# A half tile of keys whose rounded part and rest share one product, with the odd last key added by VectorE

## The chip, the cores and the metric

The kernel runs on one core of a Trainium2 chip. Its time is device time in microseconds (us), the median of several executions. Lower is better.

## What is computed

A gated block: cross-attention of 4 x 256 tokens over 1601 context rows of 256 features, then a feed-forward part in fp8 (e4m3).

```python
scores = einsum('bsd,bmd->bsm', layernorm(x), ctx) / sqrt(256)      # b=4, s=256, m=1601, d=256
scores = where(mask, scores, -1e30)
x = x + tanh(g_xattn) * (softmax(scores) @ ctx)                     # zero where no key is allowed
gate, up = e4m3(layernorm(x)) @ e4m3(w_gating[0]), ... @ e4m3(w_gating[1])   # 256 -> 1024
x = x + tanh(g_ffn) * (e4m3(gelu(gate) * up) @ e4m3(w_linear))      # 1024 -> 256
```

## The kernel before

Each batch element `b` has two tiles of 128 queries, so there are eight query tiles `j` (0 to 7, `b = j // 2`). The 1601 keys are 12 full tiles of 128 and a tail of 65, padded to 66. Four full tiles make a group `g` (0, 1, 2); the tail is group 3. To keep float32 accuracy at the speed of the rounded type fp32r, each operand is split in a rounded part (hi) and a rest (lo), and each product is made of three: hi x hi, hi x lo and lo x hi.

Each engine runs a list of steps written out by hand, one string per engine, `PE_ORDER` and its like (lines 56 to 100). `SP_ORDER` is the order of the loads on SyncE's DMA queue, and `BANK_ORDER` gives each transposing step one of three PSUM banks (`ring`) in turn. The steps are:

- `C b:i` turns the context of batch `b` (keys on partitions) into `cT` (features on partitions): TensorE transposes into a ring bank (line 773), ScalarE writes the rounded part (line 512), VectorE the rest (line 645). `C b:6` is the tail: two transposes of a 66 x 128 block. Some `C` steps of batches 2 and 3 are turned by VectorE instead (steps `D`, line 639). `X` does the same for the normalised queries.
- `A` and `S` are the score products (lines 787 to 808), `M` on VectorE adds the mask and takes the maximum (line 660), `E` on ScalarE is the exponential over all 1601 keys with its sum (line 527).
- `P j:g` transposes the weights of softmax, group by group (line 773), and splits them into `pT_hi` and `pT_lo`. `P j:3` is the tail: one transpose of a 128 x 65 block.
- `R` (ScalarE, line 519) and `Z` (GpSimd, line 461) split the context itself into hi and lo (`chl`).
- `V j:g` (`weigh`, lines 815 to 835) accumulates weights times context in PSUM (`pv`): per key tile one product of each kind, lines 824, 828 and 832. `V j:3` is the tail: three products with 65 rows of contraction.
- `A j` on VectorE (`add_attention`, lines 665 to 679) scales `pv` and adds it to `x` (line 678). `V j+1:0` waits for it (`pv_used`), since there is one `pv`.
- `B 0:g` spreads the first batch's mask over the partitions: a product with one row of contraction (line 744).
- `U`, `Q`, `L`, `N` are the second layernorm: VectorE, GpSimd (lines 451 to 454), ScalarE (line 560) and TensorE with ScalarE (lines 771 and 567). `H` are the 16 products of the first feed-forward layer (line 853) with gelu (line 575) and the multiplication (line 692), `Y` the eight of the second (line 869), each followed by line 697 and a store.
- `W` and `I` round the weights of the feed-forward part (VectorE, GpSimd).

The built program marks each product with the part of TensorE's array that it uses. Those of line 744, with one row, carry 32 x 128; all others, those with 65 and 66 rows and the transposes of 65 columns too, carry 128 x 128.

Of the kernel before, what the change touches and what calls it, by code (L numbers as in the profile page):

```python
# [5 lines left out]
def gated_cross_attention_ffn(  # L6
# [25 lines left out]
    TAIL = K - NF * P  # L32
    TPAD = TAIL + TAIL % 2
    KPAD = NF * P + TPAD
    GT = 4
# [21 lines left out]
        X0:0 W2 C0:0 W2 X0:1 C0:1 W2 A0:0 A1:0 C0:2 C0:3 A1:1 C0:4 A0:1 C0:5 B0:1 S0:1 C0:6 B0:2 B0:0 S1:1  # L57
        B0:3 C1:0 C1:1 S0:2 S0:3 X1 C1:3 S1:2 S1:3 C1:2 C1:4 C1:5 S2:0 S3:0 P0:1 P0:2 P0:0 S2:1 P1:1 P1:0
        C1:6 V0:0 S3:1 V0:1 P0:3 P1:3 V0:2 S2:2 X2 V0:3 P1:2 S2:3 V1:0 V1:1 S3:2 S3:3 S4:0 P2:1 V1:2 P2:2
        S5:0 V1:3 P2:0 C2:6 S4:1 S5:1 P3:0 P3:3 P3:1 V2:0 V2:1 P2:3 S4:2 X3 V2:2 V2:3 P3:2 S4:3 S5:2 S5:3  # L60
        V3:0 V3:1 P4:0 V3:2 V3:3 P4:2 C3:6 S6:0 P4:1 V4:0 S6:1 V4:1 P4:3 V4:2 P5:3 S6:2 S6:3 P5:1 P5:0 V4:3
        S7:0 S7:1 P5:2 S7:2 S7:3 P6:3 N0 V5:0 V5:1 N1 P6:1 P6:0 V5:2 V5:3 P6:2 P7:0 V6:0 P7:1 H0 V6:1 V6:2
        V6:3 H1 P7:2 P7:3 V7:0 V7:1 V7:2 V7:3 H2 N2 H3 H4 H5 H6 N3 H7 H8 H9 H10 H11 Y0 H12 Y1 H13 H14 H15 Y2
# [23 lines left out]
        F0 B0 Z0:0 Z0:3 F1 Z0:2 Z0:1 F3 Z1:3 Z1:1 F2 I0 Z1:2 I1 Z1:0 I2 Z2:1 Z2:3 Z2:0 Z2:2 Z3:2 Q1 Z3:3 Q0  # L87
        Z3:1 Z3:0 I3 I4 Q2 Q3 I5"""
# [828 lines left out]
```

## Time and profile before

| | us |
|---|---|
| median of 3 executions | 126.16 |
| lowest and highest | 125.7, 126.9 |
| the profiled execution | 126.15 |
| its span, first to last instruction | 124.4 |
| TensorE busy in it | 120.5 (97%) |
| VectorE busy | 97.1 (78%) |
| ScalarE busy | 87.7 (71%) |
| GpSimd busy | 82.5 (66%) |

The granted TensorE clock was 1.000 over the whole span. PE is TensorE's multiplying, PEld its loading of stationary operands, which normally runs beside the product in front. DVE is VectorE, ACT ScalarE, POOL GpSimd, SP SyncE. The record of one product is longer than the pace at which products follow each other, since they are pipelined; so durations of TensorE are read here as distances, from the chain of work, and not as mean lengths of records.

### The profile page before, as it was taken

The numbers are of one execution on the slowest core, as the hardware profiler recorded it, in microseconds if no ns is written. First come the engines' busy times: TensorE is split into PE (matmuls) and PEld (weight loads), VectorE is DVE, ScalarE is ACT, GpSimd is POOL, SyncE is SP. The second block draws the span as 40 slices with busy tenths as digits, with TensorE's granted clock in tenths as the row PEclk, the third lists the DMA queues.
The fourth block names the chain that finished last, engine by engine and source line by source line (L and its number), as shares of the span: only waits on it lengthen the run. The fifth ranks groups of instructions, "written<-read, shape, count | busy, mean of one in ns | idle before, by whom it ended". The sixth has DMA issues, their size and how long they took to land.

```text
span 124.4 us, 2562 instructions
## 1 busy us (share of the span) xinstructions
PE 120.5 (97%) x860; PEld 104.3 (84%) x860; DVE 97.1 (78%) x210; ACT 87.7 (71%) x155; POOL 82.5 (66%) x143
## 2 busy tenths in 40 slices
PE   6999999999999999999999999999999999999991
PEld 4798689887999998899999999899988984355780
DVE  3656699899999999997997796792778967666661
ACT  4288999996959969959867987969572339872400
POOL 3399399692995999199995984969519817920000
DMA  3959798679959999689717100000140000001133
GB/s 97 319 201 329 286 313 263 110 131 373 196 81 234 119 362 165 94 123 330 234 31 122 21 0 0 3 5 0 12 156 0 5 0 0 3 0 47 42 127 127
DMA packets 34439, 15.73 MB, mean 127 GB/s; under 512 B 26229, under 2 KB 33018, under 8 KB 34426
## 3 DMA queue, kind: packets, MB, share of 16 engines
q1 hardware_dynamic: 34424, 15.57, 49.5%
q8 instruction: 7, 0.11, 0.4%
q14 instruction: 6, 0.05, 0.2%
q10 hardware_dynamic: 2, 0.00, 0.0%
HBM read 14.52 MB, written 1.05 MB: 125 GB/s over the span
## 4 chain that ended last, share of the span: by engine, by line
PE 93%; ACT 3%; DVE 1%; issue 1%; ACTq 0%
PE ring L773 16%; PE pv L824 10%; PE pv L832 10%; PE pv L828 10%; PE scores L787 9%; PE scores L791 9%; PE scores L790 9%; PE scores L853 6%; PE ring L869 6%; PE pv L813 3%; ACT gate L575 2%; ACT x2T L567 1%; PE ring L744 1%; PE scores L808 1%; PE scores L804 1%; PE scores L807 1%
## 5 line engine op out<-in xcount | busy, mean ns | idle before, releaser
L461 POOL TENSOR_TENSOR chl<-cn,chl 128x256 fp32r<-128x256 f32 (+1 forms) x52 | 37.5, 754 | 5.0 <-ACT chl L519 5.0
L645 DVE TENSOR_TENSOR pT_lo<-ring,pT_hi 128x512 fp32r<-128x512 f32 (+1 forms) x32 | 18.0, 579 | 4.6 <-ACT pT_hi L512 4.4
L512 ACT ACTIVATE pT_hi<-ring 128x512 fp32r<-128x512 f32 (+1 forms) x32 | 15.5, 511 | 8.0 <-PE ring L773 8.0
L645 DVE TENSOR_TENSOR cT_lo<-ring,cT_hi 128x512 fp32r<-128x512 f32 (+1 forms) x28 | 17.0, 629 | 4.9 <-ACT cT_hi L512 4.6
L469 POOL TENSOR_TENSOR ws<-ws,wc 128x256 f32<-128x256 f32 x24 | 15.4, 678 | 7.9 <-DVE wc L687 7.9
L791 PE MATMUL scores<-cT_hi,xT_lo 128*128 128x512 f32 (+2 forms) x60 | 20.1, 342 | 0.0
L790 PE MATMUL scores<-cT_lo,xT_hi 128*128 128x512 f32 (+2 forms) x60 | 20.0, 342 | 0.0
L824 PE MATMUL pv<-chl,pT_hi 128*128 128x256 f32 (+1 forms) x104 | 18.9, 294 | 0.0
L832 PE MATMUL pv<-chl,pT_lo 128*128 128x256 f32 (+1 forms) x104 | 17.5, 281 | 0.0
L828 PE MATMUL pv<-chl,pT_hi 128*128 128x256 f32 (+1 forms) x104 | 17.4, 280 | 0.0
L787 PE MATMUL scores<-cT_hi,xT_hi 128*128 128x512 f32 (+2 forms) x60 | 16.9, 363 | 0.0
L512 ACT ACTIVATE cT_hi<-ring 128x512 fp32r<-128x512 f32 (+1 forms) x28 | 14.7, 548 | 2.9 <-PE ring L773 1.9
L472 POOL TENSOR_TENSOR wq<-ws,wc 128x256 bf16<-128x256 f32 x24 | 15.4, 672 | 0.5
L773 PE MATMUL ring<-ident,sp 128*128 128x128 f32 (+1 forms) x104 | 15.2, 273 | 0.0
L824 PEld LDWEIGHTS pv<-chl,pT_hi 128*128 128x128 f32 (+1 forms) x104 | 14.7, 189 | 0.4
L828 PEld LDWEIGHTS pv<-chl,pT_hi 128*128 128x128 f32 (+1 forms) x104 | 14.6, 189 | 0.0
L832 PEld LDWEIGHTS pv<-chl,pT_lo 128*128 128x128 f32 (+1 forms) x104 | 14.5, 188 | 0.0
L519 ACT ACTIVATE chl<-cn 128x1024 fp32r<-128x1024 f32 (+1 forms) x16 | 13.9, 892 | 0.7 <-PE pv L832 0.7
L527 ACT ACTIVATE sp<-sp,nb,sr 128x1601 f32<-128x1601 f32 x8 | 13.8, 1729 | 0.3
L773 PEld LDWEIGHTS ring<-ident,sp 128*128 128x128 f32 (+1 forms) x104 | 12.1, 140 | 1.4 <-DVE pT_lo L645 0.5
L791 PEld LDWEIGHTS scores<-cT_hi,xT_lo 128*128 128x128 f32 x60 | 11.3, 188 | 1.3
L790 PEld LDWEIGHTS scores<-cT_lo,xT_hi 128*128 128x128 f32 x60 | 11.3, 188 | 1.2
(85 smaller groups left out, 210.4 us busy)
## 6 DMA issues: line engine op xcount, KB each, us to landing
cn<-in_ctx_dram SPq DMA_DIRECT2D x11, 512.0 KB, 6.2
ws<-in_L_ffn_w_gating_dram SPq DMA_DIRECT2D x4, 512.0 KB, 4.4
raw<-in_ctx_dram SPq DMA_DIRECT2D x24, 64.0 KB, 3.0
act<-in_ctx_dram SPq DMA_DIRECT2D x24, 64.0 KB, 3.7
ws<-in_L_ffn_w_linear_dram SPq DMA_DIRECT2D x2, 512.0 KB, 4.1
out_dram<-xs SPq DMA_DIRECT2D x8, 128.0 KB, 1.7
mrow<-in_mask_BxS_bk_dram SPq DMA_DIRECT2D x3, 200.1 KB, 5.6
cn<-in_ctx_dram SPq DMA_DIRECT2D x2, 256.0 KB, 3.3
```

What stands on the lines that cost most here:

```text
L461: last = nc.gpsimd.tensor_tensor(chl[b % 2][0:parts, t, D:2 * D], cn[b % 2][0:parts, t, :], chl[b % 2][0:parts, t, 0:D].bitcast(f32), ALU. ...
L469: last = nc.gpsimd.tensor_tensor(ws[:, i % 2, c], ws[:, i % 2, c], wc[:, c], ALU.add)
L472: last = nc.gpsimd.tensor_tensor(wq[:, i, c], ws[:, i % 2, c], wc[:, c], ALU.subtract)
L512: nc.scalar.activation(dst, bank_view(f, size), ACT.Copy).then_inc(hi_ready, 1)
L645: nc.vector.tensor_tensor(dst, bank_view(f, size), hi.bitcast(f32), ALU.subtract).then_inc(lo_ready, 1)
L773: last = nc.tensor.transpose(dst, src, ident[0:parts, 0:parts])
L787: nc.tensor.matmul(dst, xT_hi[:, j % (2 * QT), k, :], cT_hi[:, k, cols], start=(k == 0), stop=False)
L790: nc.tensor.matmul(dst, xT_hi[:, j % (2 * QT), k, :], cT_lo[:, k, cols], start=False, stop=False)
L791: last = nc.tensor.matmul(dst, xT_lo[:, j % (2 * QT), k, :], cT_hi[:, k, cols], start=False, stop=(k == KD - 1))
L824: nc.tensor.matmul(pv[:, 0:D], hi[0:parts, t, :], chl[b % 2][0:parts, t, 0:D], start=(t == 0), stop=False)
L828: nc.tensor.matmul(pv[:, 0:D], hi[0:parts, t, :], chl[b % 2][0:parts, t, D:2 * D], start=False, stop=False)
L832: last = nc.tensor.matmul(pv[:, 0:D], lo[0:parts, t, :], chl[b % 2][0:parts, t, 0:D], start=False, stop=(t == NT - 1))
```

## The change

The tail's 65 keys are taken as 64 and 1.

- **The 64 keys.** `P j:3` transposes 128 x 64. The rounded weights go to partitions 0 to 63 of one block and the rest to partitions 64 to 127 of the same block. `R` rounds 128 partitions of the tail, and the load brings the 64 context rows twice, to partitions 0 to 63 and 64 to 127. `V j:3` is now two products: one with 64 rows of contraction (hi x lo), one with 128 rows, in which the hi and lo weights stand under each other against the doubled rounded context.
- **The odd key.** Its context row lies on all partitions in `crow` (steps `O` on SyncE's queue, and a first small load on ScalarE's). After each exponential ScalarE copies the odd key's weight to `podd`. `A j` gets a VectorE instruction in front of its last one, which adds `podd` times `crow` to `pv`.
- **The scores** still want `cT` of 66 columns: `C b:6` is now four transposes, two of 64 rows and two of 2 rows (odd key and a copy), in the order 64, 2, 64, 2.
- Two memsets of VectorE go. Some small tensors share memory with others.
- All orders are redrawn. The steps are the same but for the new `O0` to `O3` on SyncE's queue. The four `B0` steps now stand in four places of TensorE's order; before, two of them were neighbours.

```diff
     PE_ORDER = """
-        X0:0 W2 C0:0 W2 X0:1 C0:1 W2 A0:0 A1:0 C0:2 C0:3 A1:1 C0:4 A0:1 C0:5 B0:1 S0:1 C0:6 B0:2 B0:0 S1:1
-        B0:3 C1:0 C1:1 S0:2 S0:3 X1 C1:3 S1:2 S1:3 C1:2 C1:4 C1:5 S2:0 S3:0 P0:1 P0:2 P0:0 S2:1 P1:1 P1:0
...
+        X0:0 W2 C0:0 C0:1 W2 X0:1 W2 A0:0 A1:0 C0:3 C0:2 A1:1 B0:1 A0:1 B0:0 C0:5 C0:6 S0:1 C0:4 B0:2 S1:1
+        X1 C1:2 S0:2 B0:3 S0:3 C1:3 C1:1 C1:0 S1:2 S1:3 C1:5 C1:4 S2:0 S2:1 P0:0 P0:1 P1:1 S3:0 V0:0 C1:6
+        P0:3 P1:0 S3:1 P0:2 S2:2 S2:3 V0:1 P1:2 S3:2 V0:2 V0:3 S3:3 X2 P2:0 V1:0 P1:3 V1:1 P2:3 S4:0 V1:2
+        V1:3 P2:2 S5:0 S4:1 S5:1 C2:6 P2:1 P3:0 P3:1 V2:0 P3:2 S4:2 X3 S4:3 V2:1 V2:2 V2:3 S5:2 P3:3 S5:3
+        V3:0 V3:1 V3:2 P4:0 V3:3 S6:0 P4:1 S6:1 P4:2 V4:0 P4:3 V4:1 C3:6 V4:2 V4:3 P5:1 S6:2 S6:3 P5:3 P5:2
...
     SP_ORDER = """
-        X1 C1:0 C1:3 C1:1 C1:2 C2:3 X2 W0 M1 C2:0 T2:0 W1 C2:2 C2:1 T2:1 C3:1 C3:3 T2:2 C3:2 W2 M2 T3:0 T3:1
-        W3 C3:0 M3 W4 T3:2 W5"""
+        X1 W0 C1:3 C1:1 O1 C1:0 C1:2 M1 X2 C2:0 T2:0 C2:3 W1 T2:1 M2 O0 C2:2 M3 C3:3 T2:2 W2 C2:1 O2 T3:0
+        T3:1 C3:0 C3:1 C3:2 T3:2 W3 O3 W4 W5"""
...
             if f[0] == "P":
+                t0, t1, parts = group(f[2])
+                if f[2] == NG - 1:
+
+                    t = pT_hi[f[1] % 2]
+                    return t[0:parts, NF, :] if hi else t[parts:2 * parts, NF, :], (parts, P)
...
+                    for half in (slice(0, HALFT), slice(HALFT, P)):
+                        sp_eng.dma_start(cn[b % 2][half, NF, :], ctx_2048[b, NF * P:ODD, :]).then_inc(c_in[b % 2][g], 16)
...
+            def load_odd(b):
+
+                rows = slice(TPAD - HALFT if b < 2 else 0, P)
+                if b >= 2:
+                    sp_eng.wait_ge(pv_used, QT * (b - 1))
+                    sp_eng.wait_ge(filled, n_filled[("C", b - 2, CF - 1)])
+                sp_eng.dma_start(crow[rows, b % 2, :], ctx_2048[b, ODD:K, :].broadcast_to(
+                    [rows.stop - rows.start, D])).then_inc(odd_in[b % 2], 16)
...
                 nc.scalar.activation(sp[:, j % 2, 0:K], sp[:, j % 2, 0:K], ACT.Exp, bias=nb[:, j:j + 1],
                                      scale=sr[:, j:j + 1], accum_out=rs[:, j:j + 1]).then_inc(exp_ready, 1)
+                actor.wait_ge(exp_ready, n_exp[("E", j)])
+                nc.scalar.activation(podd[:, j:j + 1], sp[:, j % 2, ODD:K], ACT.Copy).then_inc(odd_kept, 1)
...
                 dve.wait_ge(pv_done, j + 1)
+                link(nc.vector.scalar_tensor_tensor(out=pv[:, 0:D], in0=crow[:, b % 2, :], scalar=podd[:, j:j + 1],
+                                                    in1=pv[:, 0:D], op0=ALU.mult, op1=ALU.add))
...
-                        todo = [(bank[:, k * TPAD:(k + 1) * TPAD], cn[b % 2][0:TPAD, NF, k * P:(k + 1) * P], TPAD)
-                                for k in range(KD)]
+                        todo = [(bank[:, k * TPAD + a:k * TPAD + z], rows[:, k * P:(k + 1) * P], z - a) for k in range(KD)
+                                for a, z, rows in ((0, HALFT, cn[b % 2][0:HALFT, NF, :]),
+                                                   (HALFT, TPAD, crow[0:TPAD - HALFT, b % 2, :]))]
...
+                if g == NG - 1:
+
+                    pe.wait_ge(c_lo, n_clo[("Z", b, g)])
+                    nc.tensor.matmul(total, hi[0:parts, NF, :], chl[b % 2][0:parts, NF, D:2 * D],
+                                     start=False, stop=False)
+                    pe.wait_ge(lo_ready, n_lo[f])
+                    nc.tensor.matmul(total, hi[:, NF, :], chl[b % 2][:, NF, 0:D], start=False,
+                                     stop=True).then_inc(pv_done, 1)
+                    return
```

## Rows read from the trace of the kernel before

**Rows 1.** The page, busy time, share of the span and instructions by engine.

```profile
PE 120.5 (97%) x860; PEld 104.3 (84%) x860; DVE 97.1 (78%) x210; ACT 87.7 (71%) x155; POOL 82.5 (66%) x143
```

**Rows 2.** The page, chain that ended last, shares of the span.

```profile
PE 93%; ACT 3%; DVE 1%; issue 1%; ACTq 0%
```

**Rows 3.** The waits, of PEld: waited for, us in total, times, longest.

```profile
PEld pv L813 <- DVE gate L700: 1.0, 1, 1.0
...
PEld ring L744 <- issue: 0.5, 2, 0.4
```

**Rows 4.** Chain in order of time, 11 to 18 us: start, us, what.

```profile
11.79 0.44 PE ring L773 x4
12.23 0.32 PE ring L744
12.55 0.66 PE scores L787 x2
...
14.26 0.54 PE ring L744 x2
14.79 0.66 PE scores L787 x2
...
16.38 0.13 PE ring L744
16.51 1.02 PE ring L773 x8
```

**Rows 5.** The same chain elsewhere, products with no one-row product before them.

```profile
24.32 0.47 PE scores L787 x2
...
30.36 0.47 PE pv L828 x4
...
48.46 0.56 PE ring L773 x6
...
88.83 0.88 PE ring L773 x8
...
91.59 0.86 PE scores L853 x4
```

**Rows 6.** Timeline of PE at a tail step of `weigh`.

```profile
47.94 0.28 PE L824 MATMUL pv<-chl,pT_hi 65*128 65x256 f32 x1
48.06 0.28 PE L828 MATMUL pv<-chl,pT_hi 65*128 65x256 f32 x1
48.18 0.28 PE L832 MATMUL pv<-chl,pT_lo 65*128 65x256 f32 x1
```

**Rows 7.** Groups by line and form: xcount, busy us, mean ns, idle before.

```profile
L678 DVE SCALAR_TENSOR_TENSOR xs<-pv,fo,xs 128x256 f32<-128x256 f32 x8 | 3.9, 483 | 2.1 <-PE pv L832 1.6 <-DVE fo L676 0.3
...
L525 ACT ACTIVATE nb<-mx,nsr 128x1 f32<-128x1 f32 x8 | 2.3, 292 | 0.3 <-DVE mx L660 0.2
```

**Rows 8.** Busy time by stretch: us, PE, PEld, DVE, ACT, POOL, clock, DMA.

```profile
20.00:40.00 20.00, 20.00 (x146) 18.32 (x145) 18.87 (x42) 16.95 (x33) 14.87 (x26) 1.00 0.90 200
40.00:60.00 20.00, 20.00 (x148) 18.83 (x147) 18.43 (x39) 16.95 (x29) 17.04 (x27) 1.00 0.96 202
```

**Rows 9.** Timeline of all engines at the last `A` step and behind.

```profile
101.81 0.48 DVE L678 SCALAR_TENSOR_TENSOR xs<-pv,fo,xs 128x256 f32<-128x256 f32 x1 [1.12 <-PE pv L832]
...
103.93 0.59 PE L853 MATMUL pv<-x2T,wq 128*128 128x512 fp8e4 x2
...
104.42 0.19 POOL L454 TENSOR_SCALAR nmr<-mr 128x2 f32<-128x2 f32 x1
...
105.06 1.08 ACT L560 ACTIVATE xn<-xs,nmr,rstd 128x256 fp8e4<-128x256 f32 x2
```

**Rows 10.** DMA issues: KB each and median us from issue to landing.

```profile
raw<-in_ctx_dram SPq DMA_DIRECT2D x24, 64.0 KB, 3.0
...
mrow<-in_mask_BxS_bk_dram SPq DMA_DIRECT2D x3, 200.1 KB, 5.6
...
xs<-in_x_dram SPq DMA_DIRECT2D x2, 128.0 KB, 2.1
```

More of the change, by code:

```diff
@@ L31, in gated_cross_attention_ffn @@
     NT = NF + 1
-    TAIL = K - NF * P
-    TPAD = TAIL + TAIL % 2
-    KPAD = NF * P + TPAD
+    HALFT = P // 2
+    ODD = K - 1
+    assert ODD == NF * P + HALFT
+    KPAD = K + 1
+    TPAD = KPAD - NF * P
     GT = 4
@@ L159, in gated_cross_attention_ffn @@
         pT_hi = [sb(f"pT_hi{i}", [P, NT, P], f32r) for i in range(2)]
-        pT_lo = [sb(f"pT_lo{i}", [P, NT, P], f32r) for i in range(2)]
+        pT_lo = [sb(f"pT_lo{i}", [P, NF, P], f32r) for i in range(2)]
         mrow = sb("mrow", [P, 2, K], u8)
@@ L180, in gated_cross_attention_ffn @@
         gate = sb("gate", [P, 2, HALF], bf16)
+        crow = sb("crow", [P, 2, D], f32)
         warm = gate[:, 0, 0:BANK // 2]
+        ones0 = gate[0:1, 0, BANK // 2:BANK // 2 + P]
         mrow0 = mrow[0:1, 0, :]
         brow0 = bias[0:1, 1, :]
-        ones0 = sb("ones0", [1, P], bf16)
         ident = sb("ident", [P, P], f32)
@@ L209, in gated_cross_attention_ffn @@
         fo = sb("fo", [P, J], f32)
+        podd = sb("podd", [P, J], f32)
         w1 = wq[:, 0:4, :].rearrange("p (g k) h -> p g k h", g=2)
@@ L477, in _ @@
                                     pattern=[[-1, P]], channel_multiplier=1).then_inc(ident_ready, 1)
-            nc.gpsimd.memset(ones0[:], 1.0).then_inc(row_ready, 1)
+            nc.gpsimd.memset(ones0, 1.0).then_inc(row_ready, 1)
             link(nc.gpsimd.memset(half_pow[:], -0.5))
@@ L700, in _ @@
             nc.vector.memset(warm, 0.0).then_inc(warm_ready, 1)
-            nc.vector.memset(cn[0][64:96, NF, :], 0.0).then_inc(pad_zero, 1)
-            nc.vector.memset(cn[1][64:96, NF, :], 0.0).then_inc(pad_zero, 1)
             for s in dve_order:
@@ L743, in fill @@
                     cols = mask_cols(f[2])
-                    nc.tensor.matmul(bank[:, 0:cols.stop - cols.start], ones0[:], brow0[:, cols],
+                    nc.tensor.matmul(bank[:, 0:cols.stop - cols.start], ones0, brow0[:, cols],
                                      start=True, stop=True).then_inc(filled, 1)
@@ L759, in fill @@
                     wait_ctx(pe, b, g, k)
+                    if g == NG - 1:
+                        if b < 2:
+                            pe.wait_ge(odd2_in, 16)
+                        else:
+                            pe.wait_ge(odd_in[b % 2], 16 * (b // 2 + 1))
                     if b == 0 and g == 0:
@@ L818, in weigh @@
                     pe.wait_ge(pv_used, j)
+                total = pv[:, 0:D]
                 t0, t1, parts = group(g)
@@ L827, in weigh @@
                 for t in range(t0, t1):
-                    nc.tensor.matmul(pv[:, 0:D], hi[0:parts, t, :], chl[b % 2][0:parts, t, D:2 * D],
+                    nc.tensor.matmul(total, hi[0:parts, t, :], chl[b % 2][0:parts, t, D:2 * D],
                                      start=False, stop=False)
@@ L831, in weigh @@
                 for t in range(t0, t1):
-                    last = nc.tensor.matmul(pv[:, 0:D], lo[0:parts, t, :], chl[b % 2][0:parts, t, 0:D],
-                                            start=False, stop=(t == NT - 1))
-                if g == NG - 1:
-                    last.then_inc(pv_done, 1)
+                    nc.tensor.matmul(total, lo[0:parts, t, :], chl[b % 2][0:parts, t, 0:D],
+                                     start=False, stop=False)
             def hidden(i):
```

81 lines of the change are left out of this document (43 added, 38 removed).

## The prediction

> **What bounds the kernel now.** I read the page first: TensorE is busy 97% of the span, VectorE 78%, ScalarE 71% [rows 1]. The chain that ended last says the same more sharply, 93% of it is TensorE's own work [rows 2]. The waits show how little is left: TensorE's loading of operands waited 1.0 us for the first memset, 0.5 us before the one-row products of line 744 for nothing that the profile shows, and the rest in pieces of at most 0.6 us [rows 3]. So a redrawn order can give back some tenths of a microsecond, hardly more. The time is the sum of TensorE's products at their pace, and each change to that list counts in full. VectorE is the second engine: of the 40 us from 20 to 60 it was busy 37.3 (18.87 + 18.43), which leaves it 2.7 us [rows 8].
>
> **The pace of the products.** Read from the chain, without waits: a 256-column product of `weigh` 0.47 / 4 = 0.117 us, a 128-column transpose 0.88 / 8 = 0.11, two score products 0.47, a 512-column product of bf16 or fp8 0.86 / 4 = 0.215; six transposes, of which two have 66 columns, 0.56, so (0.56 - 4 x 0.11) / 2 = 0.06 for one of the small ones [rows 5]. A tail product of 65 rows is no dearer: starts 0.12 apart [rows 6].
>
> **What a product on part of the array costs.** Line 744 is the one place where a product has less than 65 rows. The chain [rows 4] gives it 0.32 us where its columns take 0.215, and the two score products behind it 0.66 instead of 0.47. A visit (into the small part and back) costs 0.105 + 0.19 = 0.30. At the second place two such products take 0.54 instead of 0.43 and the pair behind again 0.66: 0.11 + 0.19 = 0.30, for one visit of two products. At the third the 65-column product takes 0.13, of which some 0.03 is its columns (65 of 512 x 0.215), and eight transposes 1.02 instead of 0.88: 0.10 + 0.14 = 0.24. The mean is 0.28 us a visit, 0.14 a change of part. The reading: a load for another part isn't made beside the product in front, and the new part waits until the old one is empty. The Trainium skill, TensorEngine Tiling, Tiling Modes, says that changing the tiling mode drains the engine, and lists 64 rows as a mode of its own; by that rule this change pays at each 64-row product, and the trace's wait at one row agrees with it. No row here shows 64 rows.
>
> **The change, part by part.**
> 1. *The tail of `weigh`.* One product of three goes, eight times: 8 x 0.117 = -0.94 us, all on the path. The first of the two left has 64 rows between neighbours of 128. Ends: 0, if it goes like 65 rows [rows 6], and 8 x 0.28 = +2.24, if it is a visit like line 744 [rows 4]. In size it is nearest to 65 rows, in kind (half the array is enough for it, as a part is for one row) to line 744. I take +2.24: the 65-row products use the whole array, and so show nothing of a part.
> 2. *`C b:6`.* Two transposes of 66 become 64, 2, 64, 2. The columns streamed are the same; the two extra ones cost at least the 0.03 of the smallest product seen, together 0.06. Changes of part: five (to 64, 2, 64, 2 and back), 5 x 0.14 = 0.70. With four batches 4 x 0.76 = +3.04. Ends: +0.24 with no cost of a change, and 4 x (5 x 0.19 + 0.06) = +4.04 if each change costs the dearer half of a visit.
> 3. *`P j:3`.* The stationary operand has 64 columns for 65. Nothing small there is in the trace, and a transpose of 65 columns runs at the common pace. Ends 0 and 8 x 0.28 = +2.24. I take 0, since its rows stay 128 and rows are what line 744 lacked. By the Trainium skill, TensorEngine Tiling, Restrictions, column tiling cannot be had with the transpose mode for fp32, which points to 0 as well, and by the row on line 744 alone it would be +2.24.
> 4. *Mask spreading.* Four separate visits for three: +0.28.
> 5. *`A j` on VectorE.* One more 256-element instruction of 0.483 [rows 7] and its link, about 0.04: 0.52 each, 4.2 in all. Cover: between `V j:3` and `V j+1:0` the new order always has TensorE work of over 0.9 us, and the banks it needs come from VectorE, which has idle time, though little from 20 to 60 us (2.7 against 2 x 0.52 there [rows 8]). At 0, as a slower TensorE gives more slack; were the cover gone, `A 0` to `A 3`, which lie where VectorE is full, would cost up to 4 x 0.52 = 2.1. At the end, `A 7` is done at 102.29 and the product that wants its bank starts at 103.93: covered. Behind it the second layernorm: GpSimd ended at 104.61 and ScalarE took it up at 105.06 [rows 9], slack 0.45 against 0.52: +0.07.
> 6. *`podd` on ScalarE.* 0.29 for a one-column instruction [rows 7], plus the wait for the exponential, eight times 0.35 = 2.8 us. ScalarE was idle 6.1 of the 40 us from 20 to 60 [rows 8]. What stands behind it are the rounded halves of the banks, each up to 0.35 late. At 0; bound 8 x 0.35.
> 7. *Loads.* Two issues for a tail instead of one, four for odd rows, one on ScalarE's queue before its first work: 0.5 us each on queues with idle time. The odd row of batch 2 is the narrow one: it is issued after `A 1`, and `C2:6` wants it. TensorE's cover from `V1:3` to there is `P2:2`, `S5:0`, `S4:1`, `S5:1`, about 0.44 + 3 x 1.4 = 4.6 us (six products of 0.235 per step). Needed: `A 1` about 1.1, issue 0.5, landing 2.1 to 5.6, nearest row 3.0 [rows 10]: 4.6. At 0; bound 7.2 - 4.6 = 2.6. `O0` stands behind two block loads, and `A 0` wants it; bound 1.5, half of a landing.
> 8. The two memsets of VectorE lie before its first data: 0. The shared memory adds no wait on the path: 0.
>
> **Sum.** -0.94 + 2.24 + 3.04 + 0.28 + 0.07 = +4.7. The profiled execution took 126.15, of which the span is 124.4 and 1.75 lies around it; the median is 126.16. So 126.15 + 4.7 = 130.9 us.
>
> **Rivals.**
> - *Columns count too* (part 3 at its upper end): 130.9 + 2.24 = 133.1. For it: 64 columns are half the array as 64 rows are. Against: line 744 has all its columns, so no row shows it.
> - *Only one kind counts.* If 64 rows go like 65, `C b:6` still has two visits to the 2-row part: -0.94 + 4 x (2 x 0.28 + 0.06) + 0.28 + 0.07 = +1.9, 128.0 us. If instead fp32 transposes always take the whole array, `weigh` alone pays: -0.94 + 2.24 + 0.24 + 0.28 + 0.07 = +1.9, the same 128.0.
> - *No cost for fp32 at all; not slower.* One mechanism: line 744 is bf16 and waited for its kind, and 64 and 2 rows of fp32 are loaded beside the product in front. Then -0.94 + 0.24 + 0.28 + 0.07 = -0.35, 125.8 us. For it: the part without a price in the trace. Against: on the way back the late ones were line 787's and 773's, which are fp32 [rows 4]. It decides if a change of part costs under 0.35 / 36 = 0.01 us (36 changes: 16 in `weigh`, 20 in `C b:6`).
> - *VectorE becomes the bound.* Without the changes' cost the two extra instructions per batch fall on its full stretch: 125.8 + 2.1 = 127.9 at most, 127 halfway. For it: 2.7 us of idle. Against: the order is redrawn around them.
>
> **Chances.** Forecast 0.42; columns too 0.20; one kind 0.18; no cost 0.15; VectorE 0.05. The predicted time is the first. The range must leave out no more than 0.2: it drops "no cost" and "VectorE" (0.20), begins a little under 128.0 and ends a little over 133.1, which also takes in most of a late odd row: 127.5 to 133.9. If the forecast's own case holds, 129.5 to 132.5. One per cent (1.3 us) is about what a measurement of this kernel tells from no change. Faster by over 1% would want the no-cost case and a better order besides: 0.08. Within 1%: the rest of that case and part of VectorE's: 0.12. Slower: 0.80.
>
> **What would show it.** Right: in the chain after, the product behind each 64-row product of `weigh` starts late, so that the two take about 0.23 + 0.28 = 0.51 where three took 0.35; a `C b:6` takes about 0.9 in place of 0.12; the loads of operands show waits for "issue" before and behind them; busy TensorE shares fall by some points with VectorE less full. Wrong: starts 0.12 apart through `V j:3` (then no visit exists, and the no-cost rival holds), a late transpose behind or before `P j:3` (columns count), or a new wait of TensorE for `pv_used`, for a bank or for the odd row with more than 0.5 us in total.

## The result and the profile after

| | before | after |
|---|---|---|
| median, us | 126.53 | 132.85 |
| lowest and highest of 4 executions | 125.7, 126.96 | 132.6, 133.06 |
| the profiled execution | 126.15 | 132.84 |
| its span | 124.4 | 131.1 |

The ratio is 1.051, 95% interval 1.046 to 1.057. The changed kernel is 6.3 us slower, where 4.7 had been forecast, and lies inside the range given. The granted TensorE clock was 1.00 here too. Medians and ranges, here and below, are of all executions of a kernel; the ratios leave out the few slow ones, over 1.5% above the fastest of their kernel.

The page of the changed kernel, busy time by engine and the shares of the chain that ended last, against [rows 1, 2]:

```profile
PE 124.9 (95%) x860; PEld 104.8 (80%) x860; DVE 102.4 (78%) x216; ACT 89.8 (69%) x163; POOL 82.4 (63%) x143
...
PE 86%; DMA 6%; DVE 2%; issue 1%; ACT 1%; SPq 1%; POOL 1%; DVEq 0%
```

TensorE has as many records as before and its busy share falls from 97% to 95%. The busy time still rises, since the records at the visits are longer: 0.38 us for a tail product of `weigh` where [rows 6] has 0.28. New in the chain are 6% of DMA, the early load that is treated at the end of the experiments.

The built program of the changed kernel marks the eight 64-row products of `weigh` and the 64-row transposes 64 x 128, the 2-row transposes 32 x 128 and the transposes of `P j:3` 128 x 64.

The chain of the changed kernel around `V1:3` (start, us, what; 867 and 870 are its two products), against [rows 5, 6]:

```profile
49.01 0.47 PE pv L882 x4
49.48 0.31 PE pv L867
49.79 0.32 PE pv L870
50.11 0.44 PE ring L813 x4
...
54.52 0.23 PE scores L831
54.75 2.16 PE ring L813 x16
```

In the chain, which counts from end to end, the product with 64 rows takes 0.31 us and the one with 128 rows behind it 0.32, where starts were 0.12 apart in [rows 6]. So `V j:3` costs 0.63 us in the chain for 0.35, a product fewer: a visit to the smaller part costs 0.63 - 0.235 = 0.39. All eight places look alike (in the timeline, starts 0.21, 0.31 and 0.23 apart into, through and out of the 64-row product, each 0.12 without it: 0.09 + 0.19 + 0.11 = 0.39). The last row holds the tail step `C2:6` (4 transposes) and 12 full ones: 2.16 - 12 x 0.11 = 0.84 us for what took 0.12, so +0.72. The timeline of all engines of the changed kernel shows that step from within:

```profile
54.68 0.13 PEld L813 LDWEIGHTS ring<-ident,cn 64*128 64x128 f32 x1 [0.36 <-issue]
54.68 0.27 PE L813 MATMUL ring<-ident,cn 64*128 64x64 f32 x1
54.88 0.13 PEld L813 LDWEIGHTS ring<-ident,crow 2*128 2x128 f32 x1
54.88 0.22 PE L813 MATMUL ring<-ident,crow 2*128 2x2 f32 x1
55.03 0.13 PEld L813 LDWEIGHTS ring<-ident,cn 64*128 64x128 f32 x1
55.03 0.27 PE L813 MATMUL ring<-ident,cn 64*128 64x64 f32 x1
55.23 0.13 PEld L813 LDWEIGHTS ring<-ident,crow 2*128 2x128 f32 x1
55.23 0.22 PE L813 MATMUL ring<-ident,crow 2*128 2x2 f32 x1
55.38 0.43 PEld L813 LDWEIGHTS ring<-ident,sp 128*128 128x128 f32 x4
```

Each load of a stationary operand starts at the same time as its own product. Here nothing is loaded ahead from one part of the array to the next, so each change of part puts a load on the path: starts 0.20, 0.15, 0.20 and 0.15 apart. Whether the array is also emptied first can't be seen in these records.

The other parts of the change, as groups by line and form of the changed kernel (xcount | busy us, mean ns | idle before):

```profile
L712 DVE SCALAR_TENSOR_TENSOR pv<-crow,podd,pv 128x256 f32<-128x256 f32 x8 | 3.9, 489 | 4.3 <-PE pv L870 3.4 <-ACT podd L552 0.7
...
L813 PE MATMUL ring<-ident,sp 128*64 128x128 f32 x8 | 2.2, 275 | 0.0
...
L552 ACT ACTIVATE podd<-sp 128x1 f32<-128x1 f32 x8 | 1.6, 203 | 0.3
```

and the same stretches as in [rows 8] (us, PE, PEld, DVE, ACT, POOL, clock, DMA):

```profile
20.00:40.00 20.00, 19.91 (x139) 18.03 (x139) 18.14 (x39) 18.74 (x38) 18.22 (x32) 1.00 0.83 170
40.00:60.00 20.00, 20.00 (x139) 17.98 (x139) 17.87 (x37) 15.04 (x27) 13.97 (x21) 1.00 0.67 140
```

VectorE is busy 36.0 of these 40 us, less than the 37.3 of before, in spite of its extra instructions. So it follows TensorE and hardly holds it up (run 9 puts a number on that).

**Where the time went.** I cut the trace of each kernel at the first product of every step of TensorE's order, and added up the time from one step's start to the next by kind of step (for the last step, to the end of the span). These are sums worked out from the timeline. Of a visit, the 0.09 of entering falls on the step in front.

| kind of step | before | after | difference |
|---|---|---|---|
| `X`, `W`, full `C`, `A` and the start (first microseconds) | 15.74 | 17.35 | +1.61 |
| `B` (mask) | 0.98 | 1.08 | +0.10 |
| `C b:6` | 0.55 | 2.79 | +2.23 |
| `V j:3` | 3.03 | 4.30 | +1.27 |
| the other `V` | 35.21 | 36.00 | +0.79 |
| `S` and `P` | 44.05 | 44.60 | +0.55 |
| `N`, `H`, `Y` | 24.80 | 24.95 | +0.15 |

Together +6.7, the difference of the two profiled executions (132.84 - 126.15). The +0.79 of the other `V` is mostly the entering of seven of the eight visits (7 x 0.09 = 0.63; `V3:3` stands behind `P4:0`): in kernels whose `V j:3` doesn't begin with a 64-row product these steps take 35.0 to 35.3 in either order, but for run 2 (35.8) and run 8 (36.8), where TensorE waits for others.

### The profile page after: what moved, and what is told of

It is laid out like the page before. It is cut to its first block, busy times and chain, and to the rows that moved or that the text cites. A ratio compares the mean times of both kernels' runs of the same rounds, so it can differ in the third digit from the quotient of the medians.

```text
span 131.1 us, 2595 instructions
## 1 busy us (share of the span) xinstructions
PE 124.9 (95%) x860; PEld 104.8 (80%) x860; DVE 102.4 (78%) x216; ACT 89.8 (69%) x163; POOL 82.4 (63%) x143
## 4 chain that ended last, share of the span: by engine, by line
PE 86%; DMA 6%; DVE 2%; issue 1%; ACT 1%; SPq 1%; POOL 1%; DVEq 0%
PE ring L813 16%; PE pv L874 9%; PE scores L827 9%; PE pv L882 9%; PE pv L878 9%; PE scores L831 8%; PE scores L830 8%; DMA cn<-in_ctx_dram 6%; PE scores L901 5%; PE ring L917 5%; PE pv L870 2%; PE pv L867 2%; PE ring L778 1%; ACT gate L599 1%; SPq L364 1%
## 5 line engine op out<-in xcount | busy, mean ns | idle before, releaser
L483 POOL TENSOR_TENSOR chl<-cn,chl 128x256 fp32r<-128x256 f32 (+1 forms) x52 | 38.1, 766 | 7.4 <-ACT chl L541 7.4
L673 DVE TENSOR_TENSOR pT_lo<-ring,pT_hi 128x512 fp32r<-128x512 f32 x24 | 15.7, 682 | 2.9 <-ACT pT_hi L534 2.8
L827 PE MATMUL scores<-cT_hi,xT_hi 128*128 128x512 f32 (+2 forms) x60 | 17.4, 372 | 0.0
L874 PE MATMUL pv<-chl,pT_hi 128*128 128x256 f32 x96 | 16.2, 291 | 0.0
L882 PE MATMUL pv<-chl,pT_lo 128*128 128x256 f32 x96 | 15.2, 281 | 0.0
L878 PE MATMUL pv<-chl,pT_hi 128*128 128x256 f32 x96 | 15.2, 281 | 0.0
L599 ACT ACTIVATE gate<-scores 128x512 bf16<-128x512 f32 x12 | 7.0, 594 | 9.9 <-PE scores L901 9.8
L874 PEld LDWEIGHTS pv<-chl,pT_hi 128*128 128x128 f32 x96 | 13.3, 189 | 0.3
L878 PEld LDWEIGHTS pv<-chl,pT_hi 128*128 128x128 f32 x96 | 13.0, 189 | 0.0
L882 PEld LDWEIGHTS pv<-chl,pT_lo 128*128 128x128 f32 x96 | 13.0, 189 | 0.0
```

The source lines that it names most:

```text
L483: last = nc.gpsimd.tensor_tensor(chl[b % 2][0:parts, t, D:2 * D], cn[b % 2][0:parts, t, :], chl[b % 2][0:parts, t, 0:D].bitcast(f32), ALU. ...
L673: nc.vector.tensor_tensor(dst, bank_view(f, size), hi.bitcast(f32), ALU.subtract).then_inc(lo_ready, 1)
L827: nc.tensor.matmul(dst, xT_hi[:, j % (2 * QT), k, :], cT_hi[:, k, cols], start=(k == 0), stop=False)
L874: nc.tensor.matmul(total, hi[0:parts, t, :], chl[b % 2][0:parts, t, 0:D], start=(t == 0), stop=False)
L878: nc.tensor.matmul(total, hi[0:parts, t, :], chl[b % 2][0:parts, t, D:2 * D], start=False, stop=False)
L882: nc.tensor.matmul(total, lo[0:parts, t, :], chl[b % 2][0:parts, t, 0:D], start=False, stop=False)
```

## The experiments

There are twelve runs, each measured beside the kernel before; a run's number is that of its section (9 holds two). "Changed" is the changed kernel. "The rest of the span" is the span without the first row of the table above, in which an early load plays its own part (below). By this sum before has 108.6 and changed 113.7: +5.1. It agreed within 0.1 us in the one kernel that was profiled twice (run 9), and that is all that is known of its scatter.

### 1. The tail transposes back to 66 rows

```diff
-                        todo = [(bank[:, k * TPAD + a:k * TPAD + z], rows[:, k * P:(k + 1) * P], z - a) for k in range(KD)
-                                for a, z, rows in ((0, HALFT, cn[b % 2][0:HALFT, NF, :]),
-                                                   (HALFT, TPAD, crow[0:TPAD - HALFT, b % 2, :]))]
+                        todo = [(bank[:, k * TPAD:(k + 1) * TPAD], cn[b % 2][0:TPAD, NF, k * P:(k + 1) * P], TPAD)
+                                for k in range(KD)]
```

> The changed kernel, with C b:6 as it was: two transposes of 66 rows, read from the tail's tile. Left out: the odd key's context row in the scores (its two columns repeat the first keys of the tail). Theory (each change of the array's part costs, at 64 and at 2 rows): in the changed kernel's trace the four transposes take 2 x (0.202 + 0.149) = 0.70 us a batch against 0.14 before, so this is 2.2 us faster than the changed kernel, 130.6, and the two take 0.06 each. Rival (the load order and VectorE are what costs, and the transposes only look long because they wait): less than 0.5 us comes back. Also looked at: whether the last of the 16 parts of the context's second load lands at about 7.6 us, as before, or at 9.9, as in the changed kernel.

Measured: 130.43 us (130.23 to 130.81), ratio 1.031 (1.027 to 1.036). That is 2.1 to 2.4 less than changed (132.55 when measured again, and 132.85). The four `C b:6` took 0.49 us together for 2.79, and the eight `V j:3` stayed at 4.29. With the edges 4 x 0.72 = 2.9 should come back. Not all of it arrived. TensorE, now earlier, waited longer for the odd rows: the starts into `C2:6` and `C3:6` are 0.63 and 0.58 us apart, some 0.7 more in all than in changed. The waits and the group of the small transposes in this kernel:

```profile
PE ring L812 <- DMA crow<-in_ctx_dram: 0.5, 2, 0.3
...
L812 PE MATMUL ring<-ident,cn 66*128 66x66 f32 x8 | 1.2, 230 | 0.5 <-DMA crow<-in_ctx_dram 0.5
```

The 230 ns are the length of a record, of pipelined products. So the alternating parts of `C b:6` are a cause, of about the size forecast for them.

### 2. Both tail products of `weigh` on 128 rows

```diff
-                    nc.tensor.matmul(total, hi[0:parts, NF, :], chl[b % 2][0:parts, NF, D:2 * D],
-                                     start=False, stop=False)
                     pe.wait_ge(lo_ready, n_lo[f])
+                    nc.tensor.matmul(total, hi[:, NF, :], chl[b % 2][:, NF, D:2 * D],
+                                     start=False, stop=False)
```

`Z` makes the rest of the tail on all 128 partitions. The first product then also multiplies the lo weights by the rest of the context, a small term that the other kernels leave out.

> The changed kernel, with both products of V j:3 over 128 rows: the rest of the doubled context on all 128 rows too, so that the first product also adds rest x rest. Theory of parts: both products go at 0.118, the pair 0.24 in place of 0.54: 8 x 0.30 = 2.4 us faster than the changed kernel, 130.4. Rival (a product of 64 rows is slow in itself, or the wait is for the rest of the weights, not for a part): the pair stays over 0.40 and less than 1.2 us comes back.

Measured: 130.13 us (128.92 to 130.6), ratio 1.030 (1.024 to 1.035), 2.4 to 2.7 less than changed. The eight `V j:3` took 1.98 us for 4.30, and starts are 0.12 apart again into, through and out of them, so the visits' 8 x 0.39 = 3.1 are gone. The same number of columns went through, and only the rows differ. Some 0.6 was lost again to the odd rows (starts into `C2:6` and `C3:6` 0.59 and 0.66 apart, 0.32 each in changed), one of which stands in the chain of this kernel:

```profile
49.34 3.07 DMA crow<-in_ctx_dram
```

### 3. The order 64, 64, 2, 2

```diff
-                        todo = [(bank[:, k * TPAD + a:k * TPAD + z], rows[:, k * P:(k + 1) * P], z - a) for k in range(KD)
+                        todo = [(bank[:, k * TPAD + a:k * TPAD + z], rows[:, k * P:(k + 1) * P], z - a)
                                 for a, z, rows in ((0, HALFT, cn[b % 2][0:HALFT, NF, :]),
-                                                   (HALFT, TPAD, crow[0:TPAD - HALFT, b % 2, :]))]
+                                                   (HALFT, TPAD, crow[0:TPAD - HALFT, b % 2, :])) for k in range(KD)]
```

> The changed kernel, with the four transposes of C b:6 in the order 64, 64, 2, 2 in place of 64, 2, 64, 2: same products, three changes of part for five. Theory (the price is by change, 0.14 us): 4 x 2 x 0.14 = 1.1 us faster than the changed kernel, 131.7. Rival (each small product costs in itself): no difference, 132.85.

Measured: 131.74 us (131.12 to 133.07), ratio 1.043 (1.036 to 1.050), 0.8 to 1.1 less than changed (132.55 or 132.85). The `C b:6` took 1.88 us for 2.79: -0.91 for eight changes of part less, 0.11 each. The same four transposes in another order cost less, so the changes are paid, and not only the number of small products. The medians alone would not carry this, as the intervals of the two ratios overlap a little (1.036 to 1.050, and 1.047 to 1.057 for changed in run 9); the four places in the trace do, 0.47 us each for 0.70. Two small ones of one size follow each other at 0.11 (64 rows) and 0.09 (2 rows) here, where the 66-row transposes take about 0.06, so a part of the price stays without a change. In the profiled execution most of it went back in one wait, which the timeline of this kernel shows:

```profile
56.52 0.66 PE L813 MATMUL ring<-ident,sp 128*128 128x128 f32 x4 [0.58 <-DVE cT_lo L673]
```

VectorE had not yet emptied the bank that `P3:1` takes. The rest of the span is 113.8 here, as in changed: in this execution the gain of the four steps was lost again, while the median is about 1 us lower.

### 4. Before, with 64 rows in the second product of the tail

```diff
+                few = P // 2 if g == NG - 1 else P
                 for t in range(t0, t1):
-                    nc.tensor.matmul(pv[:, 0:D], hi[0:parts, t, :], chl[b % 2][0:parts, t, D:2 * D],
+                    nc.tensor.matmul(pv[:, 0:D], hi[0:few, t, :], chl[b % 2][0:few, t, D:2 * D],
```

It leaves out one key in the product of the hi weights with the rest of the context, for the tail.

> The kernel before, with the second of the three products of V j:3 cut to 64 rows: a product of 64 rows between two of 65. Left out: the odd key in that product. Theory of parts: one visit a tail step, 8 x 0.28 to 0.30 = 2.2 to 2.4 us slower than before, 128.8. Rival (64 rows go like 65): no difference, 126.5.

Measured: 129.57 us (129.12 to 130.12), ratio 1.024 (1.019 to 1.030), +3.0 against 126.53 and +3.1 against the 126.47 beside it, where 128.8 had been expected. Its timeline of PE at the step of [rows 6]:

```profile
49.04 0.28 PE L824 MATMUL pv<-chl,pT_hi 65*128 65x256 f32 x1
49.25 0.38 PE L829 MATMUL pv<-chl,pT_hi 64*128 64x256 f32 x1
49.56 0.39 PE L833 MATMUL pv<-chl,pT_lo 65*128 65x256 f32 x1
49.78 0.38 PE L773 MATMUL ring<-ident,sp 128*128 128x128 f32 x2
```

One row fewer moves the starts from 0.12 apart to 0.21, 0.31 and 0.22: 0.39 a visit, the same as in the changed kernel, and 8 x 0.39 = 3.1. The eight `V j:3` took 6.13 us for 3.03. This is the cleanest of the runs, since nothing else of the change is in it; the built program marks these eight products 64 x 128 and the 65-row ones 128 x 128. It shows the mechanism and also that the forecast's 0.28 a visit was too little.

### 5. Before with the new orders

```diff
-        X0:0 W2 C0:0 W2 X0:1 C0:1 W2 A0:0 A1:0 C0:2 C0:3 A1:1 C0:4 A0:1 C0:5 B0:1 S0:1 C0:6 B0:2 B0:0 S1:1
+        X0:0 W2 C0:0 C0:1 W2 X0:1 W2 A0:0 A1:0 C0:3 C0:2 A1:1 B0:1 A0:1 B0:0 C0:5 C0:6 S0:1 C0:4 B0:2 S1:1
...
```

All the orders of the change, less the steps `O`.

> The kernel before with all orders of the changed kernel, less the steps O that it has no use for. Theory (the orders cost little in themselves): one more visit for the mask, +0.1 to +0.3, and no more than 0.5 us of late operands, so 126.6 to 127.3. Rival (the 1.5 us that the steps' sums leave between the kernels, outside the tail steps and the first microseconds, come from the order): 128.

Measured: 125.88 us (125.67 to 128.71, ten executions) against 126.18, ratio 0.996 (0.993 to 0.9995), a little under the 126.6 to 127.3 that had been expected. By the traces the rest of the span went from 108.6 to 108.3. The orders are not the cause of the loss.

### 6. Changed, without the odd key's work

```diff
-                actor.wait_ge(exp_ready, n_exp[("E", j)])
-                nc.scalar.activation(podd[:, j:j + 1], sp[:, j % 2, ODD:K], ACT.Copy).then_inc(odd_kept, 1)
...
-                link(nc.vector.scalar_tensor_tensor(out=pv[:, 0:D], in0=crow[:, b % 2, :], scalar=podd[:, j:j + 1],
-                                                    in1=pv[:, 0:D], op0=ALU.mult, op1=ALU.add))
```

> The changed kernel without the odd key's work in the attention: ScalarE does not copy podd, VectorE does not add it. Left out: the odd key's part of the weighted sum. The loads of the odd rows and the eight changed transposes stay. Theory (all of it is covered): at most 0.3 us faster than the changed kernel, 132.6 to 132.9. Rival (VectorE and ScalarE are late because of it and TensorE waits in pieces of 0.1 us): 1.0 to 1.5 us faster, 131.5.

Measured: 131.47 us (131.01 to 132.17), ratio 1.040 (1.035 to 1.045), 1.1 to 1.4 less than changed by the medians. At most 0.3 had been expected, so the median is a miss and lies at the rival's 131.5. By the traces, the rest of the span fell only from 113.7 to 113.2. What the medians add to these 0.5 may lie in the first microseconds, which differ between executions of one kernel; that is not shown. Run 9 takes away VectorE's part alone.

### 7. All of the change's work, but on the whole array

```diff
-                    nc.tensor.matmul(total, hi[0:parts, NF, :], chl[b % 2][0:parts, NF, D:2 * D],
-                                     start=False, stop=False)
+                    pe.wait_ge(low_zero, 2)
                     pe.wait_ge(lo_ready, n_lo[f])
+                    nc.tensor.matmul(total, hi[:, NF, :], chl[b % 2][:, NF, D:2 * D],
+                                     start=False, stop=False)
...
-                    for half in (slice(0, HALFT), slice(HALFT, P)):
-                        sp_eng.dma_start(cn[b % 2][half, NF, :], ctx_2048[b, NF * P:ODD, :]).then_inc(c_in[b % 2][g], 16)
+                    sp_eng.dma_start(cn[b % 2][0:K - NF * P, NF, :], ctx_2048[b, NF * P:K, :]).then_inc(c_in[b % 2][g], 16)
...
+            nc.vector.memset(chl[0][HALFT:P, NF, D:2 * D].bitcast(f32), 0.0).then_inc(low_zero, 1)
+            nc.vector.memset(chl[1][HALFT:P, NF, D:2 * D].bitcast(f32), 0.0).then_inc(low_zero, 1)
```

Two products a tail as in the change, the odd key still on VectorE, but the rest of the context stands above zeros in a product of 128 rows, and the transposes are those of 66 rows. ScalarE writes the rounded half twice from one load, and the small first load on its queue is gone. `P j:3` keeps its 64 columns, and the four mask products their one row.

> The changed kernel with no product of 64 or 2 rows: C b:6 has its two transposes of 66 rows, from a tail loaded once as before; ScalarE writes the rounded tail twice, to partitions 0 to 63 and 64 to 127; the rest of the context on partitions 64 to 127 is zero, and both products of V j:3 have 128 rows. Everything is computed. Theory (the two costs are separate and add): 132.85 - 2.4 - 2.4 = 128.0, less 0.3 for the late odd rows of batches 2 and 3, which no transpose waits for any more: 127.7. Rival (behind one cost the other hides, or VectorE becomes the bound): 129.5 or more.

Measured: 126.81 us (125.95 to 128.74, ten executions), ratio 1.003 (0.999 to 1.007): 5.7 to 6.0 less than changed, and no different from before. 127.7 had been expected. Its chain at `V1:3`:

```profile
46.94 0.48 PE pv L881 x4
47.42 0.12 PE pv L867
47.53 0.12 PE pv L869
47.65 0.44 PE ring L811 x4
```

Two products at their pace, 0.12 each. `V j:3` and `C b:6` together took 2.41 us here, 7.09 in changed and 3.58 before. With runs 1, 2 and 4 this is the strongest evidence for the cause: these steps gain what the products saved are worth as soon as none of them has 64 rows or fewer. The kernel as a whole gains nothing over before, though: the rest of the span is 108.3 for 108.6, and 108.3 in run 5 with the same orders, since `S` and `P` steps took 44.9 us for 44.0 there.

### 8. The same on the old orders

The four `O` steps are put in among the old loads.

```diff
-        X0:0 W2 C0:0 C0:1 W2 X0:1 W2 A0:0 A1:0 C0:3 C0:2 A1:1 B0:1 A0:1 B0:0 C0:5 C0:6 S0:1 C0:4 B0:2 S1:1
+        X0:0 W2 C0:0 W2 X0:1 C0:1 W2 A0:0 A1:0 C0:2 C0:3 A1:1 C0:4 A0:1 C0:5 B0:1 S0:1 C0:6 B0:2 B0:0 S1:1
...
```

> The same products as e8_whole_array with the orders of the kernel before, and the four loads of odd rows put in: O0 and O1 before C2:0, O2 and O3 after M3 and T3:2. Theory (eight products of 0.117 are the whole gain, and the order of before fits): 126.5 - 0.94 + 0.1 = 125.6, a ratio of 0.993. Rival (the second VectorE instruction of A makes TensorE wait where that order leaves little between V j:3 and V j+1:0): 126.5 to 127.5.

Measured: 128.97 us (128.37 to 129.61), ratio 1.020 (1.015 to 1.024), 2.2 more than run 7 and a miss for my theory, which had 125.6. The redrawn order is worth some 0.3 us to the old kernel and 2.2 us to this one by the medians; in the traces the rest of the span is 112.1 for 108.3, in an execution that was the slowest of its six. The waits of this kernel say why (waited in total, times, longest; 714 is the last instruction of `A`):

```profile
PEld pv L873 <- DVE xs L714: 1.8, 4, 0.7
PEld pv L881 <- DVE pT_lo L675: 1.3, 1, 1.3
...
PEld ring L811 <- DVE cT_lo L675: 1.1, 3, 0.6
```

`V j+1:0` stands too close behind `V j:3` for two VectorE instructions, and VectorE, later by them, also hands over banks and halves late. This is the rival "VectorE becomes the bound" of the prediction in mechanism. The longest waits for `A` stand before `V4:0`, `V6:0` and `V7:0`, though, and not at `A 0` to `A 3`, from which its 2.1 us was worked out; that the numbers are alike is luck.

### 9. Changed again, and without VectorE's instruction alone

The kernel of the change, unaltered, as a second measure:

> The changed kernel itself once more, beside the others on one chip. The times of the kernels depend on when the context's second load lands in an execution (6.7 to 10.0 us in the ten profiles so far, with and without the change). Theory (that is chance): the median comes out somewhat lower than the first 132.85, at 132.2, with a spread of over 1 us. Rival (the changed kernel's loads are always late): 132.85 with the narrow spread of the first four executions.

Measured: 132.55 us (131.64 to 133.11, eight executions), ratio 1.052 (1.047 to 1.057). Its profiled execution took 131.64, against 132.84 in the first profile, while the rest of the span is the same (113.7 in both). The 1.2 us between two executions of one kernel all lie in the first microseconds.

```diff
-                link(nc.vector.scalar_tensor_tensor(out=pv[:, 0:D], in0=crow[:, b % 2, :], scalar=podd[:, j:j + 1],
-                                                    in1=pv[:, 0:D], op0=ALU.mult, op1=ALU.add))
```

> The changed kernel without VectorE's added instruction; ScalarE still copies podd. Left out: the odd key's part of the weighted sum. e7_no_odd_work took away both and came out 1.4 us faster. If VectorE's eight times 0.52 us is what makes TensorE wait: 131.5 to 131.8, near e7. If it is ScalarE's copy behind each exponential: 132.3 to 132.8, near the changed kernel. If most of e7's gain was the chance of the early load: both within 0.6 us of e10.

Measured: 132.28 us (131.54 to 132.68), ratio 1.048 (1.042 to 1.053), 0.3 less than changed, within what these intervals leave. The rest of the span is 113.5 for 113.7. Eight instructions of 0.49 us on the second-busiest engine thus cost about 0.2 us, since the order covers them. By what was written down beforehand, 132.28 beside the 131.47 of run 6 speaks for ScalarE's copy as the dearer part; the traces give the copy only 0.3 (113.2 for 113.5). Between these two readings it stays open.

### 10. On the whole array, without the odd key's work

The edits of runs 6 and 7 together:

```diff
-                    nc.tensor.matmul(total, hi[0:parts, NF, :], chl[b % 2][0:parts, NF, D:2 * D],
-                                     start=False, stop=False)
...
+                    nc.tensor.matmul(total, hi[:, NF, :], chl[b % 2][:, NF, D:2 * D],
+                                     start=False, stop=False)
...
-                nc.scalar.activation(podd[:, j:j + 1], sp[:, j % 2, ODD:K], ACT.Copy).then_inc(odd_kept, 1)
...
-                link(nc.vector.scalar_tensor_tensor(out=pv[:, 0:D], in0=crow[:, b % 2, :], scalar=podd[:, j:j + 1],
-                                                    in1=pv[:, 0:D], op0=ALU.mult, op1=ALU.add))
```

> e8_whole_array without the odd key's work in the attention (no podd copy, no VectorE instruction). Left out: the odd key's part of the weighted sum. With TensorE's products at their shortest nothing else covers that work. Theory (it then costs more than in the changed kernel): 1.0 to 1.6 us faster than e8, 125.2 to 125.8. Rival (covered as well): 126.5.

Measured: 127.04 us (125.47 to 127.69, ten executions), ratio 1.003 (0.998 to 1.007). The medians of run 7 and of this one are the same, where 1.0 to 1.6 us less had been expected. The traces tell them apart: the rest of the span is 108.3 in run 7 and 107.5 here, so by them the odd key costs about 0.8 in a kernel with a fast TensorE. Against before's 108.6 this run is 1.1 shorter, near the eight products of 0.94 us. That the medians don't show it I can't explain by more than the scatter of the first microseconds.

### 11. Before with the new orders and the mask products as neighbours

To the kernel of run 5 one exchange in TensorE's order is added:

```diff
-        X0:0 W2 C0:0 C0:1 W2 X0:1 W2 A0:0 A1:0 C0:3 C0:2 A1:1 B0:1 A0:1 B0:0 C0:5 C0:6 S0:1 C0:4 B0:2 S1:1
+        X0:0 W2 C0:0 C0:1 W2 X0:1 W2 A0:0 A1:0 C0:3 C0:2 A1:1 A0:1 B0:1 B0:0 C0:5 C0:6 S0:1 C0:4 B0:2 S1:1
```

> e5_before_new_orders with B0:1 and B0:0 made neighbours on TensorE again (A0:1 ahead of both), everything computed. Theory (one visit to a part of the array less, 0.28): 125.6 against 125.9. Rival (the swap makes a bank late and gives it back): 125.9 or more.

Measured: 126.45 us (125.9 to 127.36, twelve executions), ratio 1.002 (0.998 to 1.005), where I had expected 125.6. The visit itself is saved as forecast: from the last product of the step in front to the first behind, the two mask products with their ways in and out are 0.29 us cheaper as neighbours than apart (the `B` steps, which hold only the middle of a visit, 0.98 for 1.08). But ScalarE gets `B0:1` later and so empties the bank of `B0:0` later, and `C0:4` waits for it:

```profile
14.37 0.66 PE L773 MATMUL ring<-ident,cn 128*128 128x128 f32 x4 [0.29 <-ACT bias L533]
```

Its start is 0.46 late in all, and the rest of the span is 108.7 for 108.3. This is the rival that had been written down: the swap makes a bank late and gives the visit back. The fastest version that ran is that of run 5, by 0.4% of before and no more.

### The early load

Nothing in the list above has the 1.6 us of the first microseconds, so I read them in all traces. TensorE wants the second load of the first context at about 8.8 us. The timeline of PE in that stretch, in the changed kernel, and after it in its second run:

```profile
10.01 0.30 PE L813 MATMUL ring<-ident,cn 128*128 128x128 f32 x1 [0.90 <-DMA cn<-in_ctx_dram]
```

```profile
8.82 1.04 PE L813 MATMUL ring<-ident,cn 128*128 128x128 f32 x8
```

The chain of the first profile of the changed kernel has it as

```profile
2.63 7.24 DMA cn<-in_ctx_dram
9.87 0.14 issue
10.01 1.06 PE ring L813 x8
```

and run 4, which has no part of the change in its loads, shows the same wait in its timeline of PE:

```profile
9.45 0.85 PE L773 MATMUL ring<-ident,cn 128*128 128x128 f32 x6 [1.23 <-DMA cn<-in_ctx_dram]
```

This wait is 1.1 of the 1.6 us. The last part of that load landed between 6.7 and 10.0 us in the fourteen traces: at 7.58 before, at 9.87 and 8.60 in the two of the changed kernel. Seven traces are of kernels with the change's small first load on ScalarE's queue, and seven of kernels without. The steps `X`, `W`, full `C` and `A`, without the 4.0 us ahead of them, took 12.9 us (11.7 to 13.5) in the first seven and 11.9 (11.7 to 12.8) in the others, medians. The two overlap, one execution each, so that the small load causes the 1.0 us between them is suggested and not shown. No run had that load alone taken out or added.

## Why the prediction was right, and what it missed

**The mechanism, right.** A product with 64 rows is a visit to a part of the array, as one with a single row is. The prediction took this by kind against the nearer 65-row row [rows 6], and three runs bear it out: 64 rows alone in the kernel before cost 3.0 to 3.1 us (run 4), 128 rows in their place gave back 2.4 to 2.7 (run 2), and the change on the whole array is as fast as before (run 7). The rule of the Trainium skill, TensorEngine Tiling, Tiling Modes, that a change of mode drains the engine and that 64 rows are a mode of their own, agrees with the starts 0.21, 0.31 and 0.23 apart where they were 0.12.

**The terms, in the prediction's order.**

| term | forecast | measured in the traces |
|---|---|---|
| 1. `V j:3` | -0.94 + 8 x 0.28 = +1.30 | -0.94 + 8 x 0.39 = +2.2 |
| 2. `C b:6` | 4 x 0.76 = +3.04 | 4 x 0.72 = +2.9 |
| 3. `P j:3`, 64 columns | 0 | 0 |
| 4. the mask, and the new orders | +0.28 | -0.3 in all (run 5); the fourth visit in it +0.29 (run 11) |
| 5., 6., 7. `A`, `podd`, odd rows, the tail | +0.07 | +0.4 to +0.5 (run 6) |
| 7. the first loads | 0 | first microseconds 1.6 longer in this profile, about 1.0 by the medians of seven traces; that the loads cause it is not shown |

Without the last line the measured terms add up to 5.2 or 5.3, and the rest of the span grew by 5.1. With about 1.0 for the first microseconds they come to the 6.3 of the medians. That the 4.7 lies so near to the 5.1 is in part luck: term 1 was 0.9 too small and the odd key's part 0.4, while the new orders gave back 0.6 that no term had.

- **Term 1, mis-sized.** The step was right in kind and wrong in its price. I took the 0.28 of the one-row visits [rows 4], and a visit of a 64-row product among 256-column ones is 0.39, in the changed kernel and in run 4 alike. One-row visits had 512 columns and stood between transposes and score products. The neighbours don't make the difference: in the changed kernel `B0:1` stands between `A` products of 256 columns, and its visit costs 0.30 there too (starts 0.21, 0.32 and 0.23 for 0.12, 0.215 and 0.12). Whether the rows, the columns or the type (bf16 against fp32r) do is not settled. It cost the forecast 8 x 0.11 = 0.9 us.
- **Term 2, right.** The four transposes take 0.70 us for 0.12, the way in 0.09 and the way out about 0.04: together 0.72 for the 0.76 put down. Five changes in `C b:6` are 0.14 each, as forecast, if all of it is put down to the changes (run 3 has 0.11 for the two that it takes away).
- **Term 3, right**, and the rival *columns count too* falls: the eight transposes on a 128 x 64 part show no late product in front or behind, and an idle time of 0.0 before them. The built program does mark them 128 x 64, so the 0 isn't there for want of a column part.
- *Only one kind counts* and *no cost for fp32* fall with runs 1, 2 and 4, since `C b:6` and `weigh` each pay by themselves.
- **Term 4.** Run 11 made two mask products neighbours again and saved 0.29 at that place, so the 0.28 for the fourth visit was right. What the term lacks is the order itself: with the fourth visit in it, it gained 0.3 by the traces (0.4% by the ratio, run 5), so the redrawing is worth about 0.6, where the prediction had it at nothing.
- *VectorE as the bound* did not come true in this order (run 9: 0.2 to 0.3 us for its instruction), but came true at once in the old one (run 8: 2.2), by waits at other places than the rival named.

**What the sum lacked.** The forecast is right in its range and its mechanism; the 1.6 us between 4.7 and 6.3 come from term 1's price, which is shown, and from the first microseconds, whose cause is not. Part 7, "loads: 0", looked for slack in the queues and not at the load that TensorE waits for first. That load had landed at 7.58 us in the trace of before, an early time among the fourteen, so 1.2 us of cover stood in the profile which other executions didn't have. A forecast from one trace took it for a property of the kernel. Whether the change itself makes the load later stays open. Part 7 also put the odd rows at nothing. They were late by some 0.1 us in the changed kernel, and by 0.6 to 0.7 more as soon as TensorE got faster (runs 1 and 2).

**The signs named.** The product behind each 64-row one late: seen, 0.63 for the two where 0.51 was written. `C b:6` at about 0.9: 0.84. TensorE's share falling: seen, but by two points only; VectorE's fell from 20 to 60 us and is 78% over the whole, as before. Loads of operands waiting for "issue": seen, in the waits of the changed kernel, at the transposes (1.6 us, where the same view of before has 0.2 at line 773) and at one of the eight tails of `weigh`:

```profile
PEld ring L813 <- issue: 1.6, 6, 0.4
...
PEld pv L867 <- issue: 0.2, 1, 0.2
```

## What to carry to other kernels

Before a product's rows are cut to 64 or fewer between products of more, set the visit (0.39 us here) against the product saved (0.12): one visit costs as much as three products of 256 columns. Fill such a block to the whole array with zeros or a second copy, which cost nothing beside the product itself in run 7 (0.12 each), and where small ones are unavoidable, put those of one size side by side. Work moved to a second engine needs an order that covers it, and with it costs little: 0.2 to 0.8 us with, 2.2 more without.

## What the runs showed of the hardware

- 65 rows are free and 64 are not: starts 0.12, 0.12, 0.12 apart, and 0.21, 0.31, 0.22, in the same place of the same kernel ([rows 6] and run 4). I had expected a visit to cost what one row costs (0.24 to 0.30 in [rows 4]), and it cost 0.39.
- A part that is narrow in columns (128 x 64) cost nothing here: eight fp32 transposes at the common pace.
- Among small parts each change costs again: starts are 0.20 and 0.15 us apart in turn in the changed kernel, and 0.11 and 0.09 where two of one size follow each other (run 3).
- The last part of an early load of the context landed anywhere from 6.7 to 10.0 us in executions of nearly the same program. In the first profile of the changed kernel, 14 of its 16 parts were there by 7.55 us, and the other two came at 8.98 and 9.87. In the second profile the last came at 8.60, TensorE did not wait, and the first microseconds were 1.2 us shorter.
